# The attention rounds of a fused adaLN block: the two halves of k, the first quarters of q and their rotated parts at other steps of the round

## The chip, the cores and the metric

The kernel runs on one core of one Trainium2 chip. The metric is the device time of one execution in microseconds (us). Before the change three runs took 1324.26, 1326.85 and 1326.16 us, a median of 1326.16 us. A round is one of the sixteen passes of the causal attention described below; a step is one of a round's 36 parts. Names such as TensorE, VectorE, ScalarE, GpSimd and SyncE are the five engines (PE, DVE, ACT, POOL and SP in the profile).

## What is computed

The input is x of shape 4 x 1024 x 128. A first attention without a mask (stage A) and its projection are added to x, with modulated layer norms around them. Then comes the part that matters here, for each of 4 batch rows and each of 4 key heads h, with four query heads g that share the key head:

```
q = (x @ wq).reshape(b, t, 16, 64);  k = (x @ wk).reshape(b, t, 4, 64);  v = (x @ wv).reshape(b, t, 4, 64)
q = q * cos + neg_half(q) * sin;     k = k * cos + neg_half(k) * sin
scores = where(causal, q . k, -inf) / 8;  p = softmax(scores);  out = (p . v) @ wo
```

A routed mixture of 8 experts follows (top 2, a capacity of 512), and the sum goes out.

## The kernel before

The causal attention is 16 rounds, one for each batch row and key head, in this order, unrolled. A round has four query heads of nine steps, 36 steps in all. A step handles four 128 x 128 blocks of the lower triangle: TensorE makes their transposed scores (scoresB, L1199 and L1200, with a mask block at L1203), ScalarE takes exp (L917) and then a float16 copy, the "high" probabilities (L905), GpSimd subtracts that copy for the "low" half (L707), and five steps later TensorE multiplies both halves with the values (L1221 to L1223, twelve matmuls a step in two parts of six).

Beside this each round carries side work, an ordered list of some sixty entries. An entry is filled by TensorE into one of three PSUM banks, taken in turn, and read by VectorE or ScalarE out of it. TensorE may fill entry n only when entry n - 3 has been read (the function before). The entries are:

- max: a piece of the row maxima of a coming head (L1125, L1128), read by one VectorE reduction (L1608, or L1610 for a piece of two). EARLY puts pieces 0 to 5 at steps 4 to 8 of a head, LATE pieces 6 to 9 at steps 0 to 3 of the next head. After the last piece the ten are joined (L1634).
- row: the joined maxima, turned by TensorE at step 5 of a head (L1138) and copied by ScalarE (L897).
- k, q, r, v: the projections of the round that follows (L1113, three matmuls of 512 columns; v at L1107). k comes in two halves of 512 tokens, q in quarters (two pairs of heads, two halves of tokens); r is the quarter of q in the order that the rotation needs. VectorE reads a half of k with three instructions, each waiting for the one before (L1583, L1585, L1587), a quarter of q with one (L1597), of r with two (L1600, L1602).
- turn, out: the output projection of the round before (L1142, L1148). in2: the input of a coming batch row.

PROJ says at which step of a round each projection stands, OUTP the same for the output. side_work puts the entries of a step together, maxima first, then projection, output, in2 and row. HIGH_AT says at which step ScalarE makes the high half of the rotated k (0) and of the two pairs of q (1, 2), by high_half (L876, L878), LOW_AT at which step GpSimd makes the low half (low_half, L680, L682). SyncE then spreads them into the operands of the scores by DMA (spread_k, spread_q), between the rows of maxima (spread_row), in a fixed order.

TensorE's order inside a step is in pe_round: the scores, and then, where the step has one side entry, both parts of the values and the entry; where it has more, the first entry, a part of the values, the second entry, the other part, the rest:

```
if n == 1:
    order = parts[0:1] + parts[1:2] + todo
else:
    order = todo[0:1] + parts[0:1] + todo[1:2] + parts[1:2] + todo[2:]
```

VectorE reads the entries in the same order. At steps 3 and 5 of a head it also divides the finished output of a bank by its sums (norm: L1644, L1647), and in twelve places in rounds 0 to 8 it does a part of the second layer norm of a coming batch row (NORM_V; L1373, L1376, L1383, L1386, L1426), five of them at step 4 of rounds 0, 1, 2, 6 and 7. The first round's projections are made ahead of the rounds (PROLOGUE, which takes PROJ's entries in the order of their steps); round 15 has none.

Of the kernel before, what the change touches and what calls it, by code (L numbers as in the profile page):

```python
# [71 lines left out]
def reader(entry):  # L72
# [1 line left out]
    return READER[entry[0]]  # L74


PROJ = {0: ("k", 0), 1: ("k", 1), 3: ("q", 0, 0), 5: ("r", 0, 0), 7: ("q", 0, 1), 9: ("r", 0, 1), 11: ("v",),
        13: ("q", 1, 0), 15: ("r", 1, 0), 17: ("q", 1, 1), 19: ("r", 1, 1)}
OUTP = {21: ("turn", 0), 23: ("turn", 1), 25: ("turn", 2), 27: ("turn", 3), 30: ("out", 0), 33: ("out", 1)}

HIGH_AT = {4: 0, 12: 1, 22: 2}
LOW_AT = {5: 0, 15: 1, 25: 2}


INPUT_AT = {0: {29: (1, 0)}, 1: {31: (1, 1)}, 4: {29: (2, 0)}, 5: {31: (2, 1)}, 8: {33: (3, 0)}, 9: {29: (3, 1)}}
# [13 lines left out]
def side_work(it):  # L99
# [3 lines left out]
    for s in range(SPR):  # L103
# [4 lines left out]
        if not (last and h >= G - 2):  # L108
            now += [("max", h + 2, n) for n in EARLY.get(c, ())]
        if not last and s in PROJ:  # L110
            now.append(PROJ[s])
        if not first and s in OUTP:
# [3 lines left out]
        if c == ROW_AT and not (last and h == G - 1):  # L116
# [5 lines left out]

PROLOGUE = ([PROJ[s] for s in sorted(PROJ)] + [("max", G, n) for n in range(len(PIECES))] + [("row", G)]
            + [("max", G + 1, n) for c in sorted(EARLY) for n in EARLY[c]])
# [53 lines left out]
def build(nc, x, cT, wmod, w_qkvT, w_projT, b_proj, g1, g2, w_kv, w_o, router_w, router_b, w_exp, consts,  # L178
          cos_t, sin_t, out):
    ctx = ExitStack()  # L180
    with ctx:
# [406 lines left out]
        def _(pool):  # L588
# [86 lines left out]
            def low_half(c, n, p):  # L675

                t = (0, 1, 0)[c]
                pool.wait_ge(r_hi, 3 * n + c + 1)
                if c == 0:
                    pool.tensor_tensor(kC[0:HD, p, :], rp1[0:HD, t, :], kB[0:HD, p, :], ALU.subtract).then_inc(r_lo, 1)  # L680
                else:
                    pool.tensor_tensor(qlo[:, c - 1, :], rp1[:, t, :], qhi[:, c - 1, :], ALU.subtract).then_inc(r_lo, 1)  # L682
# [20 lines left out]
            def pool_round(it, p, first, last):  # L703
                for s in range(SPR):
                    pool.wait_ge(b_hi, it * SPR + s + 1)
                    r = s % RING
                    pool.tensor_tensor(pl[:, r, :], pf[:, r, :], ph[:, r, :], ALU.subtract).then_inc(lo_P, 1)  # L707
                    if s in LOW_AT and not last:
                        low_half(LOW_AT[s], it + 1, 1 - p)
                    if s in NORM_P.get(it, {}):  # L710
# [41 lines left out]
        def _(act):  # L752
# [112 lines left out]
            def vec_read_of(it, e):  # L865

                work = PROLOGUE if it < 0 else flat(side_work(it))
                own = [x for x in work if reader(x) == "V"].index(e)
                return own if it < 0 else start(it, "V") + own

            def high_half(c, n, p, read_at):

                act.wait_ge(side_V, read_at + 1)
                t = (0, 1, 0)[c]
                if c == 0:
                    act.activation(kB[0:HD, p, :], rp1[0:HD, t, :], ACT.Copy).then_inc(r_hi, 1)  # L876
                else:
                    act.activation(qhi[:, c - 1, :], rp1[:, t, :], ACT.Copy).then_inc(r_hi, 1)  # L878
# [28 lines left out]
            def act_round(it, p, first, last):  # L907
# [3 lines left out]
                for s in range(SPR):  # L911
# [5 lines left out]
                    act.activation(pf[:, s % RING, :], score_banks[s % SCORES], ACT.Exp).then_inc(b_exp, 1)  # L917
                    if s in HIGH_AT and not last:
                        c = HIGH_AT[s]
                        high_half(c, it + 1, 1 - p, vec_read_of(it, ROTATED[c]))  # L920
# [1006 lines left out]
```

## Time and profile before

| | us |
|---|---|
| three runs, median (lowest, highest) | 1326.16 (1324.26, 1326.85) |
| the profiled execution, its own time | 1324.32 |
| its span, first to last instruction | 1322.5 |
| TensorE busy (matmul) | 1116.2 |
| VectorE busy | 1053.8 |
| GpSimd busy | 998.5 |
| ScalarE busy | 872.8 |

All times of the trace are counted from the start of the span. In the timeline each line has the start, the length, the engine, the line of the kernel, the operation, and what is written and read; a bracket at the end gives how long the engine had been idle and what ended it. A matmul's end is modelled: the next one may start before it, so that a run of matmuls is timed by their starts. Rounds 0 to 15 fill the span from about 238 to 1110 us.

### The profile page before, as it was taken

What the parts mean: (1) busy time and instruction counts of PE and PEld (TensorE: products, weight loads), DVE (VectorE), ACT (ScalarE), POOL (GpSimd) and SP (SyncE); (2) the same over time, 40 slices, a digit from 0 to 9 for tenths busy, and PEclk for the clock granted to TensorE, in tenths of its full rate; (3) what the DMA queues carried; (4) which work ended last, traced back from release to release, by engine and by line L of the source; (5) the groups of instructions that cost most, each with busy time, mean ns of one, the idle gap of its engine ahead of it and who ended that gap; (6) DMA issues with size and microseconds to landing.
All of it is one profiled execution on the core that took longest, in us unless ns stands there. A gap on an engine that the chain in (4) does not pass through costs nothing.

```text
span 1322.5 us, 36076 instructions
## 1 busy us (share of the span) xinstructions
PE 1116.2 (84%) x14984; PEld 839.5 (63%) x14984; DVE 1053.8 (80%) x2180; ACT 872.8 (66%) x1508; POOL 998.5 (76%) x783
## 2 busy tenths in 40 slices
PE   4979895899999899999999999999999997600891
PEld 2768682566776667767677776776767776600881
DVE  6588765889888898989989889898898875592675
ACT  3656671698888688878888888887888894100330
POOL 3555874698898788989899898798888996226454
PEclk8889998899999899999999999999999999555996
DMA  6240013121222211213112131121211200022793
GB/s 219 50 140 2 2 44 86 42 77 43 71 55 56 61 38 52 58 60 77 38 52 54 49 87 43 53 61 42 77 38 26 62 3 2 0 88 74 219 303 145
DMA packets 49247, 90.85 MB, mean 69 GB/s; under 512 B 8896, under 2 KB 19136, under 8 KB 48832
## 3 DMA queue, kind: packets, MB, share of 16 engines
q1 hardware_dynamic: 46128, 81.21, 21.5%
q0 software_dynamic: 2960, 7.38, 2.1%
q8 instruction: 117, 1.92, 0.6%
q14 instruction: 42, 0.34, 0.1%
HBM read 43.96 MB, written 13.01 MB: 43 GB/s over the span
## 4 chain that ended last, share of the span: by engine, by line
PE 61%; DVE 20%; POOL 7%; issue 4%; SPq 3%; ACT 2%; DMA 2%; POOLq 0%; DVEq 0%; ACTq 0%
PE psT L1125 6%; PE psS L1200 5%; PE psS L1199 5%; PE psT L1113 5%; PE psS L1221 5%; PE psS L1222 5%; PE psS L1223 4%; PE psT L1148 3%; PE psO L1125 3%; PE psO L1200 3%; PE psO L1199 3%; DVE pmax L1608 2%; POOL rows_in L735 2%; DVE psT L1585 2%; DVE arena L1587 2%
## 5 line engine op out<-in xcount | busy, mean ns | idle before, releaser
L707 POOL TENSOR_TENSOR probs<-arena,probs 128x512 f16<-128x512 f32 x576 | 656.7, 1161 | 109.2 <-ACT probs L905 104.9
L905 ACT ACTIVATE probs<-arena 128x512 f16<-128x512 f32 x576 | 362.0, 628 | 14.1
L1221 PE MATMUL psS<-vb,probs 128*128 128x65 f16 x2304 | 302.9, 193 | 3.5 <-POOL probs L707 1.2
L1222 PE MATMUL psS<-vb,probs 128*128 128x64 f16 x2304 | 304.1, 194 | 0.0
L1223 PE MATMUL psS<-vb,probs 128*128 128x65 f16 x2304 | 302.2, 192 | 0.0
L917 ACT ACTIVATE arena<-psS 128x512 f32<-128x512 f32 x384 | 226.1, 589 | 105.9 <-PE psS L1203 59.1
L1221 PEld LDWEIGHTS psS<-vb,probs 128*128 128x128 f16 x2304 | 220.4, 97 | 71.6 <-issue 11.2
L1222 PEld LDWEIGHTS psS<-vb,probs 128*128 128x128 f16 x2304 | 215.7, 97 | 47.7 <-issue 0.5
L1608 DVE TENSOR_REDUCE pmax<-psT 128x1 f32<-128x512 f32 (+1 forms) x311 | 198.1, 641 | 28.9 <-PE psT L1128 14.1
L1223 PEld LDWEIGHTS psS<-vb,probs 128*128 128x128 f16 x2304 | 217.0, 99 | 0.0
L1125 PE MATMUL psT<-arena 128*128 128x512 f16 (+3 forms) x507 | 153.4, 323 | 8.6 <-DVE pmax L1608 4.9
L1200 PE MATMUL psS<-arena 65*128 65x512 f16 (+1 forms) x448 | 158.2, 353 | 0.0
L1199 PE MATMUL psS<-arena 128*128 128x512 f16 (+1 forms) x448 | 156.9, 350 | 0.0
L1608 DVE TENSOR_REDUCE pmax<-psO 128x1 f32<-128x512 f32 (+1 forms) x201 | 134.2, 667 | 23.9 <-PE psO L1125 16.2
L917 ACT ACTIVATE arena<-psO 128x512 f32<-128x512 f32 x192 | 112.5, 586 | 25.2 <-PE psO L1200 16.4
L1113 PE MATMUL psT<-arena,wkv 128*128 128x512 f16 x381 | 105.1, 386 | 20.8 <-DVE arena L1587 19.5
L647 POOL TENSOR_TENSOR probs<-arena,probs 128x1024 f16<-128x1024 f32 x32 | 69.4, 2172 | 55.8 <-ACT probs L847 55.7
L1199 PE MATMUL psO<-arena 128*128 128x384 f16 (+2 forms) x320 | 93.7, 293 | 0.0
L958 ACT ACTIVATE arena<-arena 128x256 f32<-128x256 f32 x40 | 16.7, 418 | 112.8 <-DVE arena L1841 112.7
L1125 PE MATMUL psO<-arena 128*128 128x512 f16 (+2 forms) x261 | 85.7, 341 | 5.4 <-DMA arena<-arena 4.6
L1200 PE MATMUL psO<-arena 65*128 65x384 f16 (+2 forms) x320 | 88.4, 295 | 0.0
L1128 PE MATMUL psT<-maskh,identh 128*128 128x128 bf16 x391 | 79.2, 220 | 0.0
(278 smaller groups left out, 2873.2 us busy)
## 6 DMA issues: line engine op xcount, KB each, us to landing
arena<-arena SPq DMA_DIRECT2D x240, 128.0 KB, 2.4
arena<-w_exp_dram SPq DMA_DIRECT2D x40, 384.0 KB, 4.1
arena<-xnT_d SPq DMA_DIRECT2D x16, 512.0 KB, 3.6
wkv<-w_d SPq DMA_DIRECT2D x16, 352.0 KB, 4.1
rows_in<-arena POOLq DMA_DIRECT2D x1, 2580.0 KB, 20.5
arena<-rows_in SPq DMA_DIRECT2D x40, 64.5 KB, 3.3
arena<-x_dram SPq DMA_DIRECT2D x4, 512.0 KB, 5.2
hres<-x_dram SPq DMA_DIRECT2D x4, 512.0 KB, 5.3
```

What stands on the lines that cost most here:

```text
L707: pool.tensor_tensor(pl[:, r, :], pf[:, r, :], ph[:, r, :], ALU.subtract).then_inc(lo_P, 1)
L905: act.activation(ph[:, s % RING, :], pf[:, s % RING, :], ACT.Copy).then_inc(b_hi, 1)
L917: act.activation(pf[:, s % RING, :], score_banks[s % SCORES], ACT.Exp).then_inc(b_exp, 1)
L1113: mm = pe.matmul(dst, wkv[:, p, c, w0:w0 + P], xs[:, p, a, h * 512:(h + 1) * 512], start=(k == 0), stop=(k == 2))
L1125: mm = pe.matmul(dst[:, k * w:(k + 1) * w], qA[:, p, g, i * P:(i + 1) * P], kC[:, p, h * 512:h * 512 + w], start=True, stop=not diag)
L1128: mm = pe.matmul(dst[:, (k + 1) * w - P:(k + 1) * w], identh[:, :], maskh[:, :], start=False, stop=True)
L1199: pe.matmul(dst, kA[:, p, j * P:(j + 1) * P], qA[:, p, g, i0 * P:(i0 + n) * P], start=True, stop=False)
L1200: mm = pe.matmul(dst, kB[0:HD + 1, p, j * P:(j + 1) * P], qB[0:HD + 1, p, g, i0 * P:(i0 + n) * P], start=False, stop=not diag)
L1221: pe.matmul(dst, high, vb[:, p, j, 0:OW], start=first, stop=False, skip_group_check=True)
L1222: pe.matmul(dst[:, 0:HD], high, vb[:, p, j, HD + 2:VW], start=False, stop=False, skip_group_check=True)
L1223: mm = pe.matmul(dst, low, vb[:, p, j, 0:OW], start=False, stop=last, skip_group_check=True)
L1608: ins = v.tensor_reduce(pmax[:, e[1] % 2, at[0]:at[0] + 1], src[:, 0:w], AX.X, ALU.max)
```

## The change

Three tables get other numbers. The first half of k stays at step 0; the second goes from step 1 to 2, the first quarter of q from 3 to 4, its rotated part from 5 to 6, the second quarter from 7 to 8; its rotated part stays at 9. ScalarE's high half of k goes from step 4 to 5, GpSimd's low half from 5 to 6. No instruction is added or taken out, and the order of the projections among themselves stays, so the prologue is unchanged. The order against the other entries changes: between the halves of k there are now two maxima and not one, and so on, and with it the bank of some entries.

```diff
-PROJ = {0: ("k", 0), 1: ("k", 1), 3: ("q", 0, 0), 5: ("r", 0, 0), 7: ("q", 0, 1), 9: ("r", 0, 1), 11: ("v",),
+PROJ = {0: ("k", 0), 2: ("k", 1), 4: ("q", 0, 0), 6: ("r", 0, 0), 8: ("q", 0, 1), 9: ("r", 0, 1), 11: ("v",),
         13: ("q", 1, 0), 15: ("r", 1, 0), 17: ("q", 1, 1), 19: ("r", 1, 1)}
 OUTP = {21: ("turn", 0), 23: ("turn", 1), 25: ("turn", 2), 27: ("turn", 3), 30: ("out", 0), 33: ("out", 1)}
 
-HIGH_AT = {4: 0, 12: 1, 22: 2}
-LOW_AT = {5: 0, 15: 1, 25: 2}
+HIGH_AT = {5: 0, 12: 1, 22: 2}
+LOW_AT = {6: 0, 15: 1, 25: 2}
```

## Rows read from the trace of the kernel before

**Rows 1.** The page's busy times: engine, us, share of the span, instructions.
```profile
PE 1116.2 (84%) x14984; PEld 839.5 (63%) x14984; DVE 1053.8 (80%) x2180; ACT 872.8 (66%) x1508; POOL 998.5 (76%) x783
```

**Rows 2.** TensorE's waits: who waited for whom, us in total, times, longest.
```profile
PE psT L1113 <- DVE arena L1587: 19.5, 17, 2.1
```

**Rows 3.** Timeline of TensorE, that wait in rounds 0 and 14.
```profile
245.07 0.82 PE L1113 MATMUL psT<-arena,wkv 128*128 128x512 f16 x3 [1.23 <-DVE arena L1587]
...
1016.53 0.82 PE L1113 MATMUL psT<-arena,wkv 128*128 128x512 f16 x3 [1.11 <-DVE arena L1587]
```

**Rows 4.** Timeline of TensorE, steps 0 to 9 of round 11.
```profile
846.58 0.39 PE L1125 MATMUL psT<-arena 128*128 128x512 f16 x1 [0.26 <-DVE pmax L1610]
846.99 0.81 PE L1113 MATMUL psT<-arena,wkv 128*128 128x512 f16 x3
847.82 0.38 PE L1199 MATMUL psS<-arena 128*128 128x512 f16 x1
848.03 0.38 PE L1200 MATMUL psS<-arena 65*128 65x512 f16 x1
...
849.54 0.38 PE L1199 MATMUL psO<-arena 128*128 128x512 f16 x1
...
850.56 0.38 PE L1199 MATMUL psS<-arena 128*128 128x512 f16 x1
...
852.67 0.82 PE L1113 MATMUL psT<-arena,wkv 128*128 128x512 f16 x3 [1.10 <-DVE arena L1587]
...
854.58 0.33 PE L1199 MATMUL psO<-arena 128*128 128x384 f16 x1
...
856.53 0.27 PE L1199 MATMUL psS<-arena 128*128 128x256 f16 x1
...
860.86 0.38 PE L1199 MATMUL psS<-arena 128*128 128x512 f16 x1
```

**Rows 5.** Timeline of VectorE, the same steps.
```profile
847.83 0.68 DVE L1583 TENSOR_TENSOR arena<-psT,trig 64x512 f32<-64x512 f32 x1
...
849.28 0.68 DVE L1587 TENSOR_TENSOR arena<-psT,arena 64x512 f32<-64x512 f32 x1
849.89 0.67 DVE L1608 TENSOR_REDUCE pmax<-psO 128x1 f32<-128x512 f32 x1
...
851.93 0.68 DVE L1587 TENSOR_TENSOR arena<-psT,arena 64x512 f32<-64x512 f32 x1
...
852.87 0.54 DVE L1608 TENSOR_REDUCE pmax<-psO 128x1 f32<-128x384 f32 x1
...
853.62 0.66 DVE L1597 TENSOR_TENSOR arena<-psT,trig 128x512 f32<-128x512 f32 x1
854.20 0.41 DVE L1647 TENSOR_TENSOR arena<-psS,oinv 128x256 f32<-128x256 f32 x1
```

**Rows 6.** Timeline of ScalarE and of GpSimd, the same steps.
```profile
854.69 1.04 ACT L876 ACTIVATE arena<-arena 64x1024 f16<-64x1024 f32 x1
...
856.34 2.42 POOL L707 TENSOR_TENSOR probs<-arena,probs 128x512 f16<-128x512 f32 x2 [2.52 <-ACT probs L905]
```

**Rows 7.** Timeline of VectorE and TensorE, norm work at step 4, rounds 2 and 1.
```profile
354.62 0.68 DVE L1426 TENSOR_TENSOR hres<-hres,rstd2a 128x512 f32<-128x512 f32 x1
...
298.49 1.21 DVE L1383 TENSOR_REDUCE st2a<-arena 128x8 f32<-128x1024 f32 x1
...
302.68 0.34 PE L1125 MATMUL psT<-arena 128*128 128x384 f16 x1 [0.52 <-DVE arena L1602]
```

**Rows 8.** Timeline of VectorE, TensorE and GpSimd, steps 24 and 25 of round 3.
```profile
440.42 4.37 DVE L1386 SCALAR_TENSOR_TENSOR st2b<-st2b,epsb 128x8 f32<-128x8 f32 x1
...
445.31 0.39 PE L1125 MATMUL psT<-arena 128*128 128x256 f16 x1 [4.69 <-DVE pmax L1608]
...
430.37 11.21 POOL L707 TENSOR_TENSOR probs<-arena,probs 128x512 f16<-128x512 f32 x10
...
443.61 1.15 POOL L707 TENSOR_TENSOR probs<-arena,probs 128x512 f16<-128x512 f32 x1
```

**Rows 9.** Busy time by stretch: TensorE, weights, VectorE, ScalarE, GpSimd; granted clock, DMA.
```profile
849.00:904.00 55.00, 53.49 (x766) 38.44 (x765) 48.16 (x92) 45.38 (x81) 47.22 (x39) 1.00 0.21 54
...
446.00:450.00 4.00, 4.00 (x30) 2.56 (x28) 3.42 (x6) 1.23 (x2) 1.16 (x1) 0.50 0.03 7
```

## The prediction, made before the changed kernel ran

> **What bounds the kernel now.** I first read the page's busy times [rows 1]: TensorE leads with 1116.2 us, but VectorE has 1053.8 and GpSimd 998.5, so a share alone names no limit. The stretches show the rounds: in the 55 us around round 11 TensorE is busy 53.49 us at a granted clock of 1.00, VectorE 48.16, GpSimd 47.22 [rows 9]. TensorE issues nearly without a hole, so a microsecond taken from its waits in a round is a microsecond of the kernel. The next view is therefore its waits. One group stands out: projections (L1113) that wait for the third instruction of a read of k (L1587), 17 times, 19.5 us [rows 2]. The timeline places them: two lie in the prologue, and one, of 1.1 to 1.2 us, stands in each of rounds 0 to 14, the rounds that carry projections [rows 3].
>
> Round 11 shows why [rows 4, 5]. Step 1 begins at 847.82, step 2 at 849.54, step 3 at 850.56. A projection and the half of the values behind it take 0.83 us of issue (846.99 to 847.82), three passes of 0.21 us (847.82 to 848.03) making 0.65 of it. So the second k is issued at 849.54 - 0.83 = 848.71, 0.89 after its step began. Step 3 is built alike but for a maximum of 384 columns, 0.05 us shorter: its quarter of q is due at 850.56 + 0.84 = 851.40. It starts at 852.67. The hole is 1.27 us (the bracket says 1.10 because the ends are modelled). It is there because this entry takes the bank of the second k, and VectorE was at that read until 852.6: a read of k is three chained instructions, 1.45 us from first to third (847.83 to 849.28), and two of them stand with one maximum between them.
>
> **The change part by part.** No instruction goes or comes, so every gain is a wait that ends earlier.
>
> *The second k at step 2.* Step 1 without it takes 1.72 - 0.65 = 1.07 us, so step 2 begins at 848.89. Its maximum and half of the values put the k at + 0.84, 849.73. Now it takes the bank of the first k (before, of a maximum). That read's third instruction starts at 849.28, and TensorE starts 0.74 us after such a start (851.93 to 852.67), at 850.02. So there is a new wait, 0.29 us. Step 3 begins 0.83 later, at 850.85.
>
> *The quarter of q at step 4.* Step 3 now looks like the old step 2, 1.02 us: step 4 begins at 851.87. The old step 4 ran from 852.67 + 0.84 to 854.58, 1.07 us with both halves of values; up to the quarter of q it takes 0.89, so this is due at 852.76. It needs the second k read. From k's issue to the first instruction is 0.84 (846.99 to 847.83), to the third 1.45, to the release 0.74: 850.02 + 3.03 = 853.05. VectorE is free for it: its two maxima behind the first k run from 849.89 and take 0.6 and 0.33 us, to 850.82, and the k arrives at 850.86. The wait is 0.29 us. Step 5 begins at 853.05 + 0.83 = 853.88 where it began at 854.58. **0.70 us is gained**: 1.27 becomes twice 0.29.
>
> *The rotated part at step 6, the second quarter at step 8.* VectorE is now late next. Step 5 took 1.95 us (854.58 to 856.53) and takes 1.30 without the rotated part; at step 6 scores, a maximum and half the values (0.95) put the rotated part at 856.13. It takes the bank of step 5's maximum. VectorE ends the second k at 852.31 + 0.61 = 852.92; a maximum, the joining and a reciprocal take 0.75 (852.87 to 853.62), the scaled output 0.5, then a maximum 0.6, the quarter of q 0.58 (853.62 to 854.20) and the maximum in question, starting at 855.33, released at 856.07. That is 0.06 us before it is needed: no wait, on a thin margin. Each further delay of VectorE would come through, so I let this term cost 0 to 0.3 us in a plain round. The second quarter at step 8 has two maxima ahead of it and is not late by the same count.
>
> *Rounds with norm work at step 4.* There VectorE has 0.6 us more (rounds 2 and 7) or a reduction of 1.21 us more (rounds 0, 1, 6) ahead of that maximum [rows 7]. For rounds 2 and 7 the thin margin becomes a wait of 0.54 us, and 0.16 us of gain is left. In the other three VectorE already makes TensorE wait again behind the rotated part (0.52 us by the bracket in round 1 [rows 7]); part of the new wait is one that was there anyhow. I bound each of them by - 0.5 and + 0.9 us and take + 0.5, nearer the upper end since that old wait disappears.
>
> *The high and low half of k.* The same copy of 1.04 us on ScalarE and the subtraction on GpSimd, one step on. On ScalarE the copy stood ahead of step 4's high probabilities; now these come first, the copy stands behind step 5's exp, and the row of maxima keeps its place behind it. GpSimd was idle 2.52 us for those probabilities [rows 6], so its catching up starts earlier, by about the 0.7 us that TensorE gains. What waits for k's halves is SyncE's three transfers (spread_k), queued ahead of a row that is only ready at step 14, and the first maximum that needs k, at step 22. That is 16 steps of cover, and I cost them nothing; without the cover each step of delay would stand in the first scores of a round.
>
> *The sum.* Plain rounds are 3, 4, 5 and 8 to 14: 10 x 0.70 = 7.0. Rounds 2 and 7: 0.3. Rounds 0, 1 and 6: 1.5. Together 8.8 us against the profiled 1324.32: 1315.5. The median of the runs, 1326.16, lies 1.8 higher and gives 1317.4; I forecast 1317.0. The bounds: 10 x 0.4 - 1.5 = 2.5 us of gain, and 19 us (15 x 1.27) if all of the wait went. I stay with the sum because the two new waits follow from durations of the same round.
>
> *One stall elsewhere.* In round 3 a VectorE instruction on 128 x 8 numbers in SBUF takes 4.37 us, ends with GpSimd's unbroken run (443.61 + 1.15), and costs TensorE 4.69 us [rows 8]; afterwards the granted clock is 0.50 [rows 9], the lower of its levels, 1.2 of 2.4 GHz. With about 5 us at half speed that is some 7.2 us. Whether it returns hangs on how its start falls against GpSimd's instructions; both move by the same 0.7 us, so I leave it in the sum. The Trainium skill, "SBUF — State Buffer", section "Who interferes with whom", says that a VectorE instruction with two SBUF inputs contends with a GpSimd one that reads SBUF, and that the one that issued second blocks until the first has finished. By that rule the wait would end with one GpSimd instruction, 1.1 us here; the row shows a wait past three of their ends, so the trace agrees on who blocks and not on how long.
>
> **The rivals.**
>
> *The stall of round 3 goes too* (0.23). For it: a shift of a tenth against GpSimd's 1.12 us beat (11.21 over ten [rows 8]) can decide. Against: the two move together. Then 1317.0 - 7.2 = 1309.8.
>
> *The wait is gone whole* (0.03): if VectorE released banks earlier than counted, 1326.2 - 19 = 1307. The chained read speaks against it.
>
> *Nothing is gained* (0.16). VectorE's work from step 0 to 9 is the same and nearly unbroken, so the old wait could come back whole behind the rotated part at step 6, or the stall of round 3 come once more in another place and take the gain: 1324.5 to 1326.5. Against: the idle between VectorE's reads in round 11, and the count above.
>
> *Slower* (0.09). Twelve pieces of the second norm run on VectorE in rounds 0 to 8, some with SBUF inputs beside a GpSimd that is seldom idle. If the moved phases add two more stalls of the kind of round 3, that is 2 x 7.2 - 8.8 = + 5.6: about 1331.8. It decides from the second on; one more only cancels the gain. Against: one of a dozen places does it now.
>
> **How the numbers follow.** The forecast has 0.49. The range goes from 1308.5 to 1323.5: it takes in the stall that goes (1309.8) and the forecast with its bounds (1326.16 - 2.5 = 1323.7 at the top), and leaves out most of no gain, the slower case and the whole wait gone. About 0.2%, or 2.7 us, is what a measurement of this kernel can tell from no change. Faster by more: 0.49 + 0.23 + 0.03 = 0.75; within: 0.16; slower: 0.09.
>
> **What would show it.** Right: in each of rounds 3 to 5 and 8 to 14 TensorE's bracket of 1.1 us is replaced by two small ones, at the second k and at the first quarter of q, both released by L1587; step 5 begins 0.7 us earlier after step 0; no bracket at the rotated part but in rounds 0, 1, 2, 6 and 7. Wrong: a bracket above 0.4 us at the rotated part (released by L1608) in plain rounds, or a stall as that of round 3 in another round. The prediction falls if the rounds keep their length although the bracket is gone.

## The result, and the profile after

The changed kernel takes 1315.28 us (median of four runs, 1314.48 to 1315.96) against 1326.47 us for the kernel before (1324.26 to 1326.85, a fourth run added to the three shown above). The ratio is 0.9916, with a 95% interval of 0.9902 to 0.993. The profiled execution took 1314.48 us with a span of 1312.7 us: 9.8 us less than before in both. It is the fastest of its four; the one before, at 1324.32 us, lies 0.06 us above the fastest run of its kernel. The forecast was 1317.0 us, 1308.5 to 1323.5, and faster.

The page of the changed kernel, to be read against [rows 1]:

```profile
PE 1115.0 (85%) x14984; PEld 837.8 (64%) x14984; DVE 1054.2 (80%) x2180; ACT 870.3 (66%) x1508; POOL 998.5 (76%) x783
```

The same work in the same number of instructions; only the span is shorter. What went is in TensorE's waits (who waited for whom, us in total, times, longest), to be read against [rows 2]:

```profile
PE psT L1113 <- DVE arena L1587: 3.5, 3, 2.1
PE psO L1113 <- DVE pmax L1608: 3.4, 5, 1.1
```

Of 17 waits for the third instruction of a read of k three are left, two of them the prologue's; the third, 0.86 us at the second k, is in round 0, where the first five steps have no values to multiply yet. In place of the others stand five, in the five rounds with norm work at step 4, released by a maximum (L1608).

Round 11 of the changed kernel, TensorE (start, length, engine, line, operation), answers to [rows 4]:

```profile
839.25 0.38 PE L1199 MATMUL psS<-arena 128*128 128x512 f16 x1
...
840.52 0.81 PE L1113 MATMUL psT<-arena,wkv 128*128 128x512 f16 x3
841.35 0.38 PE L1199 MATMUL psS<-arena 128*128 128x512 f16 x1
...
842.42 0.38 PE L1199 MATMUL psO<-arena 128*128 128x512 f16 x1
...
843.24 0.19 PE L1223 MATMUL psS<-vb,probs 128*128 128x65 f16 x1
843.56 0.82 PE L1113 MATMUL psT<-arena,wkv 128*128 128x512 f16 x3
844.40 0.38 PE L1199 MATMUL psS<-arena 128*128 128x512 f16 x1
...
845.42 0.38 PE L1199 MATMUL psS<-arena 128*128 128x512 f16 x1
...
846.61 0.82 PE L1113 MATMUL psT<-arena,wkv 128*128 128x512 f16 x3
847.45 0.33 PE L1199 MATMUL psO<-arena 128*128 128x384 f16 x1
...
848.75 0.27 PE L1199 MATMUL psS<-arena 128*128 128x256 f16 x1
...
849.71 0.81 PE L1113 MATMUL psO<-arena,wkv 128*128 128x512 f16 x3
...
893.21 0.38 PE L1199 MATMUL psS<-arena 128*128 128x512 f16 x1
```

and VectorE, which answers to [rows 5]:

```profile
842.82 0.68 DVE L1587 TENSOR_TENSOR arena<-psT,arena 64x512 f32<-64x512 f32 x1
...
844.42 0.68 DVE L1583 TENSOR_TENSOR arena<-psT,trig 64x512 f32<-64x512 f32 x1
...
845.87 0.68 DVE L1587 TENSOR_TENSOR arena<-psT,arena 64x512 f32<-64x512 f32 x1
...
848.88 0.68 DVE L1608 TENSOR_REDUCE pmax<-psO 128x1 f32<-128x512 f32 x1
```

The second k was due 0.84 us after its step began, at 843.26; it came at 843.56, 0.74 after L1587 started at 842.82. The quarter of q was due 0.89 after 845.42, at 846.31; it came at 846.61, 0.74 after 845.87. So there are two waits of 0.30 us where there was one of 1.27. Neither shows as a bracket, although the prediction named brackets as its sign: a matmul is recorded as ending up to 0.2 us after the next could be issued, so only 0.13 us of the first hole is left as idle time in the records (843.24 + 0.19 = 843.43, to 843.56), and the timeline puts no bracket on so little. Holes of this size are found by starts. Step 5 begins 6.10 us after step 1 (847.45 - 841.35); before it was 6.76 [rows 4]. The gain is 0.66 us.

Taking a round's length from its first score matmul to that of the next, round 11 took 53.96 us (893.21 - 839.25). Before, round 11 and round 12 began at

```profile
845.72 0.38 PE L1199 MATMUL psS<-arena 128*128 128x512 f16 x1
...
900.34 0.38 PE L1199 MATMUL psS<-arena 128*128 128x512 f16 x1
```

which makes 54.62 us. Worked out so for every round, the gains are 0.66 to 0.68 us in rounds 4, 5 and 8 to 14, 1.5 in round 3, 0.85 in round 1, 0.34 in round 6, 0.14 in rounds 2 and 7, - 0.14 in round 0 and none in round 15: together 8.8 us. Another 0.3 us lies before round 0 and 0.7 us after the rounds, in code that the change does not touch.

Round 3 keeps its stall, in VectorE, TensorE and GpSimd as in [rows 8]:

```profile
438.62 4.41 DVE L1386 SCALAR_TENSOR_TENSOR st2b<-st2b,epsb 128x8 f32<-128x8 f32 x1
...
443.55 0.40 PE L1125 MATMUL psT<-arena 128*128 128x256 f16 x1 [4.73 <-DVE pmax L1608]
...
428.61 11.21 POOL L707 TENSOR_TENSOR probs<-arena,probs 128x512 f16<-128x512 f32 x10
...
441.86 1.14 POOL L707 TENSOR_TENSOR probs<-arena,probs 128x512 f16<-128x512 f32 x1
```

Only the time at the lower clock behind it is shorter (busy times by stretch as in [rows 9], granted clock third from the end of the line), which is where round 3's other 0.9 us come from:

```profile
444.00:448.00 4.00, 4.00 (x43) 2.76 (x42) 3.61 (x7) 1.58 (x3) 1.07 (x1) 0.67 0.09 20
```

### The profile page after: what moved, and what is told of

Its sections match the earlier page's. It is cut to its first block, busy times and chain, and to the rows that moved or that the text cites. A ratio compares the mean times of both kernels' runs of the same rounds, so it can differ in the third digit from the quotient of the medians.

```text
span 1312.7 us, 36076 instructions
## 1 busy us (share of the span) xinstructions
PE 1115.0 (85%) x14984; PEld 837.8 (64%) x14984; DVE 1054.2 (80%) x2180; ACT 870.3 (66%) x1508; POOL 998.5 (76%) x783
## 4 chain that ended last, share of the span: by engine, by line
PE 60%; DVE 21%; POOL 7%; issue 4%; SPq 3%; ACT 2%; DMA 2%; POOLq 0%; DVEq 0%; ACTq 0%
PE psT L1125 6%; PE psS L1200 5%; PE psS L1199 5%; PE psS L1221 5%; PE psS L1222 5%; PE psT L1113 4%; PE psS L1223 4%; PE psT L1148 3%; PE psO L1200 3%; DVE pmax L1608 3%; PE psO L1199 3%; PE psO L1125 3%; POOL rows_in L735 2%; PE psO L1113 2%; DVE psT L1585 2%
## 5 line engine op out<-in xcount | busy, mean ns | idle before, releaser
L707 POOL TENSOR_TENSOR probs<-arena,probs 128x512 f16<-128x512 f32 x576 | 656.8, 1162 | 100.2 <-ACT probs L905 97.1
L905 ACT ACTIVATE probs<-arena 128x512 f16<-128x512 f32 x576 | 361.2, 627 | 14.5
L1608 DVE TENSOR_REDUCE pmax<-psT 128x1 f32<-128x512 f32 (+1 forms) x341 | 218.8, 645 | 26.1 <-PE psT L1128 13.5
L1125 PE MATMUL psT<-arena 128*128 128x512 f16 (+3 forms) x507 | 157.7, 329 | 8.3 <-DVE pmax L1608 5.2
L1608 DVE TENSOR_REDUCE pmax<-psO 128x1 f32<-128x512 f32 (+1 forms) x171 | 113.6, 664 | 18.5 <-PE psO L1125 12.3
L1113 PE MATMUL psT<-arena,wkv 128*128 128x512 f16 x336 | 92.8, 387 | 8.5 <-DVE arena L1587 3.5
L1125 PE MATMUL psO<-arena 128*128 128x512 f16 (+3 forms) x261 | 80.7, 328 | 5.1 <-DMA arena<-arena 4.7
L1128 PE MATMUL psT<-maskh,identh 128*128 128x128 bf16 x361 | 73.1, 220 | 0.0
```

Source lines behind the costliest of these rows:

```text
L905: act.activation(ph[:, s % RING, :], pf[:, s % RING, :], ACT.Copy).then_inc(b_hi, 1)
L1113: mm = pe.matmul(dst, wkv[:, p, c, w0:w0 + P], xs[:, p, a, h * 512:(h + 1) * 512], start=(k == 0), stop=(k == 2))
L1125: mm = pe.matmul(dst[:, k * w:(k + 1) * w], qA[:, p, g, i * P:(i + 1) * P], kC[:, p, h * 512:h * 512 + w], start=True, stop=not diag)
L1128: mm = pe.matmul(dst[:, (k + 1) * w - P:(k + 1) * w], identh[:, :], maskh[:, :], start=False, stop=True)
L1608: ins = v.tensor_reduce(pmax[:, e[1] % 2, at[0]:at[0] + 1], src[:, 0:w], AX.X, ALU.max)
```

## The experiments

The theory to be tested, called the bank theory: TensorE's wait is for a PSUM bank that VectorE still reads, and which entry waits follows from the order of the entries, three banks apart. Its rivals were that the distance between the two halves of k matters in itself, that thinning VectorE's reads matters, or that the later copies on ScalarE and GpSimd do. Executions differ by up to 3.6 us in the part before round 0 (the first score matmul stands between 236.95 and 240.56 us), so beside the medians I compare lengths of rounds, which do not carry that. Round 0 is an exception: experiment 9 edits rounds 2 and 3 alone, and its round 0 is still 1.06 us shorter than the changed kernel's (51.02 against 52.08), with a granted clock of 0.90 in its first part (237.84 to 241.00) against 0.68 (236.98 to 241.00). So a difference in round 0 is not laid to an edit here. Rounds are read from one traced execution of each kernel, and the runs of one kernel spread by 1.4 to 10.5 us. Each ratio is to runs of the kernel before that were taken beside it, with medians from 1325.55 to 1328.47 us, so it is the ratios that can be compared between experiments. Edits are against the changed kernel where nothing else is said.

**1. The projections alone.**

```diff
-HIGH_AT = {5: 0, 12: 1, 22: 2}
-LOW_AT = {6: 0, 15: 1, 25: 2}
+HIGH_AT = {4: 0, 12: 1, 22: 2}
+LOW_AT = {5: 0, 15: 1, 25: 2}
```

> The projections at the changed steps, the high and low half of k at their old steps 4 and 5. Bank theory (all of the gain is TensorE's wait for a bank that VectorE still reads; where ScalarE and GpSimd make the halves of k costs nothing): as the changed kernel, 1315.3 us within 1.5. Rival (the later halves keep ScalarE and GpSimd from waiting for the read of k, and part of the gain is theirs): 1318 to 1324 us, with a wait of ScalarE for L1587 in each round.

Measured: 1314.15 us (1309.02 to 1316.76), ratio 0.9905 (0.9873 to 0.9938). Round 11 takes 53.96 us, as with the whole change. But it is not the same in all rounds. Round 3 took

```profile
403.48 0.38 PE L1199 MATMUL psS<-arena 128*128 128x512 f16 x1
...
459.44 0.38 PE L1199 MATMUL psS<-arena 128*128 128x512 f16 x1
```

55.96 us against 60.31 with the change (458.87 - 398.56): its stall is short here, L1386 takes 0.94 us. And rounds 0, 1, 2 and 7 are 0.4 to 0.5 us longer than with the change. In round 2 VectorE's norm piece at step 4 (L1426) took 1.15 us where it takes 0.68 with the change; GpSimd was busy beside it. So the projections carry the gain of the plain rounds, and the moved halves of k change when GpSimd runs, which costs or gives where VectorE's norm pieces stand. The rival's sign, a wait of ScalarE for L1587 in each round, is absent: there is one, in the prologue, as in the changed kernel.

**2. The halves of k alone.** Against the kernel before:

```diff
-HIGH_AT = {4: 0, 12: 1, 22: 2}
-LOW_AT = {5: 0, 15: 1, 25: 2}
+HIGH_AT = {5: 0, 12: 1, 22: 2}
+LOW_AT = {6: 0, 15: 1, 25: 2}
```

> The projections at their old steps, the high and low half of k at the changed steps 5 and 6. Bank theory: as the kernel before, 1326.5 us within 1.5, with the bracket of 1.1 us at the first quarter of q in all 15 rounds. Rival (the halves carry part of the gain): 1318 to 1324 us.

Measured: 1325.76 us (1317.86 to 1328.35), ratio 0.999 (0.9972 to 1.0008). Round 11 takes 54.61 us (before 54.62), with the old wait:

```profile
854.45 0.82 PE L1113 MATMUL psT<-arena,wkv 128*128 128x512 f16 x3 [1.10 <-DVE arena L1587]
```

For the plain rounds the rival that gave ScalarE and GpSimd a share of the gain falls. In round 1 it does not. The halves alone make that round 0.72 us shorter (55.41 against 56.13), by as much as its small norm instruction L1386 becomes shorter, here before and in this experiment:

```profile
299.73 0.89 DVE L1386 SCALAR_TENSOR_TENSOR st2a<-st2a,epsb 128x8 f32<-128x8 f32 x1
...
302.91 0.17 DVE L1386 SCALAR_TENSOR_TENSOR st2a<-st2a,epsb 128x8 f32<-128x8 f32 x1
```

**3. The halves of k apart, q at its old steps.**

```diff
-PROJ = {0: ("k", 0), 2: ("k", 1), 4: ("q", 0, 0), 6: ("r", 0, 0), 8: ("q", 0, 1), 9: ("r", 0, 1), 11: ("v",),
+PROJ = {0: ("k", 0), 2: ("k", 1), 3: ("q", 0, 0), 5: ("r", 0, 0), 7: ("q", 0, 1), 9: ("r", 0, 1), 11: ("v",),
```

> Of the projections only the second half of k moves (step 1 to 2). Bank theory: the first quarter of q, still at step 3, now takes the bank of a maximum and does not wait; the second k waits 0.29 us for the first; a new wait of about 0.3 us comes at the maximum of step 7, behind the rotated part still at step 5. By that count 0.7 us are gained in a plain round and the time is 1316 to 1318 us. Rival (VectorE's reads have to be thinned out over the steps, so the moved quarters of q carry the gain): 1322 to 1327 us.

Measured: 1316.59 us (1313.65 to 1321.87), ratio 0.9939 (0.9916 to 0.9962). The time fell where the bank theory had it, and the median is out of the rival's 1322 to 1327. The first quarter of q, at step 3 as ever, does not wait at all: the bank it takes is now that of a maximum. Round 11 takes 54.05 us, 0.57 less than before. The new wait, though, is not at the maximum of step 7. It is at step 5, where the values write into a bank whose old content VectorE divides late, behind the reads of k and of the quarter of q:

```profile
849.36 0.19 PE L1221 MATMUL psS<-vb,probs 128*128 128x65 f16 x1 [0.23 <-DVE arena L1647]
```

My count had left that dependence out.

**4. The halves of k together, q at its new steps.** The second k back at step 1, all else as changed.

```diff
-PROJ = {0: ("k", 0), 2: ("k", 1), 4: ("q", 0, 0), 6: ("r", 0, 0), 8: ("q", 0, 1), 9: ("r", 0, 1), 11: ("v",),
+PROJ = {0: ("k", 0), 1: ("k", 1), 4: ("q", 0, 0), 6: ("r", 0, 0), 8: ("q", 0, 1), 9: ("r", 0, 1), 11: ("v",),
```

> The second half of k back at step 1, the quarters of q and the rotated part at the changed steps. Bank theory: the entry that waits for the second k is now the maximum of step 4, due 0.59 us before the release at 852.67 in the frame of round 11; 0.7 us of 1.27 are gained, 1315 to 1317 us. Rival (the distance of the two halves of k is what helps, as the name of the change has it): the wait of 1.1 us stays, 1324 to 1327 us.

Measured: 1316.99 us (1315.99 to 1318.75), ratio 0.9937 (0.9915 to 0.9959), and round 11 takes 53.96 us: the gain of a plain round is there in full, with the halves of k a single step apart. The wait is where the theory puts it, at step 4's maximum, which now takes the bank of the second k:

```profile
846.76 0.39 PE L1125 MATMUL psT<-arena 128*128 128x512 f16 x1 [0.43 <-DVE arena L1587]
```

By starts it is 0.6 us. The distance of the halves, the headline of the change, is not needed. Either move alone gives nearly all, since each puts another entry, due later, into the bank that the second k leaves.

**5. The read of the second k made longer.**

```diff
                 if kind == "k":
                     h = slice(e[1] * 512, (e[1] + 1) * 512)
+                    if e[1] == 1 and it > 0:
+                        v.tensor_reduce(spare[0:HD, it:it + 1], src[0:HD, :], AX.X, ALU.max)
```

> The changed kernel with one more VectorE reduction (64 x 512, some 0.6 us, its result not used) ahead of the read of the second half of k in 15 rounds. Bank theory (that read sets TensorE's wait at the first quarter of q): the wait grows from 0.3 to 0.9 us in each round, 15 x 0.6 = 9 us, about 1324. If VectorE has slack behind it or something else sets the wait: 1315 to 1317.

Measured: 1326.7 us (1325.35 to 1328.78), ratio 1.0011 (0.9997 to 1.0024). VectorE starts the added reduction at 852.65 and the read proper at 853.26, 0.61 us later; round 11 takes 54.56 us, 0.60 more than the changed kernel. Rounds 1, 2 and 4 to 14 are each 0.59 to 0.61 us longer, so what is added to this read TensorE waits for one to one. The median is 2.7 us above the 1324 expected; 2.3 us of the difference between the traced executions lie before and after the rounds, which the edit does not explain (the lines of this kernel are numbered one to three higher):

```profile
852.65 0.68 DVE L1585 TENSOR_REDUCE spare<-psT 64x1 f32<-64x512 f32 x1
853.26 0.67 DVE L1586 TENSOR_TENSOR arena<-psT,trig 64x512 f32<-64x512 f32 x1
...
855.43 0.82 PE L1114 MATMUL psT<-arena,wkv 128*128 128x512 f16 x3 [0.73 <-DVE arena L1590]
```

**6. q two steps later than before.** The second k is back at step 1.

```diff
-PROJ = {0: ("k", 0), 2: ("k", 1), 4: ("q", 0, 0), 6: ("r", 0, 0), 8: ("q", 0, 1), 9: ("r", 0, 1), 11: ("v",),
+PROJ = {0: ("k", 0), 1: ("k", 1), 5: ("q", 0, 0), 7: ("r", 0, 0), 9: ("q", 0, 1), 10: ("r", 0, 1), 11: ("v",),
-HIGH_AT = {5: 0, 12: 1, 22: 2}
+HIGH_AT = {5: 0, 13: 1, 22: 2}
```

> The second half of k at step 1, the first quarter of q at 5, its rotated part at 7, the second quarter at 9, its rotated part at 10; the high half of the first q at step 13. Bank theory: in a plain round only 0.22 us of wait is left, at the maximum of step 4, so about 1.0 of 1.27 us are gained, and rounds 0, 1, 2, 6, 7 lose less than in the changed kernel: about 1310 us, 1308 to 1313. Rival (VectorE's work as a whole limits the steps 0 to 10, so thinning cannot give more than the change has): 1314 to 1317 us.

Measured: 1310.88 us (1309.92 to 1312.48), ratio 0.9871 (0.9848 to 0.9895). The number is the expected one and the reason is not. Round 11 takes 54.18 us, longer than with the change and 0.44 less than before, where about 1.0 was expected: beside the small wait at step 4 the values of step 5 wait for VectorE's division again, by 0.42 us of bracket.

```profile
842.00 0.19 PE L1221 MATMUL psS<-vb,probs 128*128 128x65 f16 x1 [0.42 <-DVE arena L1647]
```

The time came from elsewhere: round 3 took 56.19 us instead of 60.31, its stall short as in experiment 1, and rounds 0, 1, 2, 6 and 7 gained 0.3 to 0.8 us each on the change. A median that lands on the forecast did not confirm the count here; the lengths of the rounds speak against it.

**7. Round 3's stall: another step.** The variance of the second norm (L1383, L1386) at step 22 of round 3.

```diff
-3: {24: ("d", 2)},
+3: {22: ("d", 2)},
```

> The changed kernel with round 3's piece of the second norm (variance, L1383 and L1386) at step 22 and not at 24. Chance theory (the small instruction L1386 comes in at the next end of a GpSimd instruction but for an unlucky moment): the wait shrinks to at most 1.2 us, TensorE's 4.7 us and the slow clock behind it go, 1308 us within 2. Backlog theory (it gets in only when GpSimd runs out of queued work): the wait stays at 4 us or more, 1314 to 1318 us.

Measured: 1317.13 us (1315.93 to 1317.31), ratio 0.9919 (0.9897 to 0.994). L1386 takes 3.03 us, from 437.23 to 440.26. GpSimd's run, in whose middle it was issued, ends at 430.13 + 10.11 = 440.24:

```profile
437.23 3.03 DVE L1386 SCALAR_TENSOR_TENSOR st2b<-st2b,epsb 128x8 f32<-128x8 f32 x1
...
430.13 10.11 POOL L707 TENSOR_TENSOR probs<-arena,probs 128x512 f16<-128x512 f32 x9
```

The nine instructions take 1.12 us each, so L1386 was issued some 0.4 us into one of them and two of their ends went by. The chance theory falls. The wait is also shorter than the 4 us or more of the backlog theory: GpSimd's run ended sooner after it.

**8. Round 3's stall: one input.**

```diff
-v.scalar_tensor_tensor(st[:, 3, :], st[:, 2, :], 1.0 / D, epsb[:, eps, :], ALU.mult, ALU.add).then_inc(n, 1)
+v.tensor_scalar(st[:, 3, :], st[:, 2, :], 1.0 / D, (LN_EPS, RMS_EPS)[eps], ALU.mult, ALU.add).then_inc(n, 1)
```

> The changed kernel with L1386 as an instruction with one SBUF input and two constants (times 1/128, plus the epsilon) in place of two SBUF inputs; the same numbers come out. If the second input from SBUF is what makes it wait for GpSimd: L1386 takes about 0.17 us in all places and the time is 1308 us within 2. If any VectorE instruction of that place waits (the second way: this form contends as well, or something else holds VectorE): about 4 us again, 1315 us within 1.5.

Measured: 1314.9 us (1314.6 to 1317.7), ratio 0.9907 (0.9883 to 0.9932); the instruction takes 4.43 us.

```profile
439.99 4.43 DVE L1386 TENSOR_SCALAR st2b<-st2b 128x8 f32<-128x8 f32 x1
```

A second input from SBUF is not needed for the wait. The Trainium skill, "SBUF — State Buffer", section "Who interferes with whom", names this form too among those that can take the pair of ports shared with GpSimd, so the run does not speak against the page's cause; it does show that this form is no way out.

**9. Round 3's stall: less queued on GpSimd.** One GpSimd piece of 2.36 us moved from round 3's step 8 to round 2's step 31.

```diff
-2: {18: ("scaled", 2)}, 3: {8: ("shifted", 2), 30: ("power", 2, 1)},
+2: {18: ("scaled", 2), 31: ("shifted", 2)}, 3: {30: ("power", 2, 1)},
```

> The changed kernel with one GpSimd piece of the second norm (2.36 us, L630) taken from round 3's step 8 to round 2's step 31. Backlog theory (L1386 waits at step 24 of round 3 because GpSimd's run behind that piece has no pause until its queued work is gone): GpSimd is 2.4 us less behind, its run has a pause before step 24, L1386 takes at most 1.2 us, and 4 to 7 us go: 1308 to 1311. Chance theory: the wait stays at about 4 us and the time at 1315.3 within 1.5.

Measured: 1312.68 us (1310.48 to 1315.41), ratio 0.9906 (0.9889 to 0.9923). The median is 1.7 us above the upper end of the range I gave. The six runs go from 1310.48, the traced one, up to 1315.41, where the chance theory had them, so whether the wait came in some of the others is not known. In the traced one it is gone. Round 3 takes 55.97 us (454.33 - 398.36), 4.3 less than with the change, and L1386 0.94:

```profile
438.41 0.94 DVE L1386 SCALAR_TENSOR_TENSOR st2b<-st2b,epsb 128x8 f32<-128x8 f32 x1
...
434.72 4.61 POOL L707 TENSOR_TENSOR probs<-arena,probs 128x512 f16<-128x512 f32 x4 [1.07 <-ACT probs L905]
439.29 2.12 POOL L682 TENSOR_TENSOR arena<-arena 128x1024 f16<-128x1024 f32 x1
```

GpSimd has caught up: it waited 1.07 us for ScalarE at 434.72, and L1386 gets in at the end of that run (434.72 + 4.61 = 439.33), although GpSimd's next instruction stood ready. The rest of TensorE's bracket, 1.25 us, is the variance itself and that wait.

**10. Both.** Experiment 9's edit, and the rest of q spread further behind the changed steps of k and of the first quarter of q.

```diff
-PROJ = {0: ("k", 0), 2: ("k", 1), 4: ("q", 0, 0), 6: ("r", 0, 0), 8: ("q", 0, 1), 9: ("r", 0, 1), 11: ("v",),
+PROJ = {0: ("k", 0), 2: ("k", 1), 4: ("q", 0, 0), 7: ("r", 0, 0), 9: ("q", 0, 1), 10: ("r", 0, 1), 11: ("v",),
-HIGH_AT = {5: 0, 12: 1, 22: 2}
+HIGH_AT = {5: 0, 13: 1, 22: 2}
```

> The edit before this one and, beside the changed steps of k and of the first quarter of q, its rotated part at step 7, the second quarter at 9, its rotated part at 10, the high half of the first q at 13. By the count of banks the plain rounds stay as in the changed kernel (two waits of 0.29 us), and the waits of 0.35 to 1.1 us at the rotated part in rounds 0, 1, 2, 6 and 7 go or fall below 0.5: some 3 us less than the edit before it, about 1306. If VectorE's work as a whole is the limit there: no gain on that edit.

Measured: 1308.25 us (1306.0 to 1312.03), ratio 0.9862 (0.9841 to 0.9882), below the change's own interval and that of experiment 9. It is the lowest here, but its interval overlaps that of experiment 6 (0.9848 to 0.9895). Some 3 us less than experiment 9 were expected; the median is 4.4 us lower, the rounds together 2.0. Round 11 takes 53.96 us as forecast, rounds 1, 2 and 7 gain 0.5 to 0.7 us each on the change, and the rounds together are 16.2 us shorter than before, against 8.8 for the change. The waits at the rotated part are gone. The two waits of 0.3 us are left, in round 0 as brackets of 0.9, and brackets of 0.4 and 0.2 us at a maximum in rounds 1 and 6.

## Why the prediction was right

**What bounds the kernel.** TensorE issues nearly without a hole in the rounds, and the hole of 1.27 us was VectorE's read of the second k. Experiments 3 and 4 show it by giving the bank of that read to another entry, experiment 5 by dose in the changed kernel: 0.61 us more of that read, 0.60 us more of round 11.

**The second k and the quarter of q.** Forecast: two new waits of 0.29 us, 0.70 us gained in a plain round. Measured: two of 0.30, and 0.66. The durations taken from one round before the change (0.84 from issue to read, 1.45 along the chain, 0.74 to release) came back in the round after it.

**The rotated part at step 6.** Forecast: needed at 0.06 us after its bank's release, no wait. Measured: released at 848.88 + 0.74 = 849.62, issued at 849.71 as due. The thin margin held.

**Norm work at step 4.** Forecast: 0.16 us of gain left in rounds 2 and 7, and 0.5 in each of rounds 0, 1 and 6, between - 0.5 and + 0.9. Measured: 0.14 twice, and - 0.14, 0.85 and 0.34, 1.05 together for the 1.5 forecast. The waits stand at the rotated part, where VectorE still reads the maximum whose bank it takes (here rounds 0, 1 and 7):

```profile
249.19 0.82 PE L1113 MATMUL psO<-arena,wkv 128*128 128x512 f16 x3 [0.71 <-DVE pmax L1608]
...
300.36 0.82 PE L1113 MATMUL psO<-arena,wkv 128*128 128x512 f16 x3 [1.08 <-DVE pmax L1608]
...
633.04 0.82 PE L1113 MATMUL psO<-arena,wkv 128*128 128x512 f16 x3 [0.35 <-DVE pmax L1608]
```

That these terms came out so near is in part luck. With the halves of k at their old steps (experiment 1) rounds 2 and 7 lose 0.33 us each, and rounds 0, 1 and 6 gain 0.2 together. The count had taken the norm piece of rounds 2 and 7 at the 0.68 us that it took before; it kept that length only because the halves had moved as well.

**The halves of k at nothing.** For the plain rounds experiments 1 and 2 show it: they keep and lose the gain without regard to these halves. For the other rounds this term failed: experiment 1 shows that, with the projections at their new steps, moving them cost 4.4 us in round 3 and gave some 0.5 us in each of rounds 1, 2 and 7, and with experiment 2 that most of round 1's 0.85 us came with them. Over all rounds the traced execution of experiment 1 is 2.6 us shorter than that of the change. The count had only asked who waits for the halves, not what GpSimd's moved work stands beside.

**The sum.** 8.8 us was forecast for the rounds and 8.8 was measured, with smaller parts cancelling: some 0.03 us less per plain round and 0.45 less in rounds 0, 1 and 6 together, against 0.8 us more in round 3 from a shorter time at the lower clock. That the two totals agree to a tenth is luck. The profiled executions differ by 9.84 us and the medians by 11.2; the 0.7 us after the rounds and the difference between medians and profiled runs are not traced further.

**The rivals.** That the wait goes whole, or comes back whole behind the rotated part, is out by the starts of round 11. The stall of round 3 stayed, as the forecast had it, with "both move by the same 0.7 us" as the ground. They did move together: L1386 was issued 10.05 us into GpSimd's run of ten before (440.42 - 430.37), 10.01 after (438.62 - 428.61), and 9.97 to 10.03 in experiments 2 to 5 and 8. That the stall stayed for this reason is not shown, and the rival's own reason, that a shift of a tenth against GpSimd's beat can decide, found no support: in experiments 7 and 9 L1386 was issued alike, 0.4 and 0.2 us into an instruction of GpSimd's, and it took 3.03 us in the one and 0.94 in the other. What differs is how long GpSimd had run without a pause, 25.9 us against 3.7. The price of 7.2 us was too high: without the stall round 3 is 4.3 us shorter than with the change (experiment 9), and TensorE keeps a bracket of 1.25 us there, which the price had counted in. No second such stall came in another round.

## What to carry to other kernels

Where a pipeline fills a few banks in turn and one reader is slow with some of them, ask for every step which entry takes the bank that is still being read, and put there one that is due late: in round 11 moving the second k alone gave 0.57 us, moving the quarters of q alone 0.66, and both 0.66. Such a plan can be counted ahead from a handful of starts and releases of one round, if every user of the slow engine is in the count: with VectorE's divisions left out, the counts of experiments 3 and 6 put the remaining wait at the wrong place. And work that is moved along off the critical path can cost or give elsewhere, as the halves of k did. A stall that happens once deserves its own look; here it was worth nearly half of what the change brought (4.3 us in round 3 of experiment 9, against 9.8 us of the span).

## What the runs showed of the hardware that was not expected

A VectorE instruction on 128 x 8 numbers in SBUF can wait for GpSimd through several of its instructions. In eight kernels (the two compared, and experiments 2 to 5, 7 and 8) L1386 of round 3 took 3.03 to 4.45 us and ended within 0.03 us of the end of GpSimd's unbroken run, past two or three ends of single instructions; where GpSimd had shortly before waited for ScalarE, it got in at the next end and took 0.93 to 0.94 us (experiments 1, 6, 9 and 10). That the one that issued second blocks until the other instruction has finished, as the Trainium skill has it ("SBUF — State Buffer", section "Who interferes with whom"), fits the second case and not the first.

Nor does queued work alone decide. In round 6 of the kernel before, the same line got in at an end inside GpSimd's run of seven (616.42 + 7.86 = 624.28) and took 0.72 us from 618.00, with two finished high halves waiting for GpSimd (by the ends of L905 and the starts of L707) where in round 3 there was one. Nor does the place within GpSimd's instruction decide: in round 8 of all twelve kernels L1386 was issued about 1.1 us into one, as in round 3 of seven of the eight, and took 0.17 us. In the changed kernel:

```profile
701.81 0.17 DVE L1386 SCALAR_TENSOR_TENSOR st2b<-st2b,epsb 128x8 f32<-128x8 f32 x1
...
698.41 4.60 POOL L707 TENSOR_TENSOR probs<-arena,probs 128x512 f16<-128x512 f32 x4 [0.50 <-ACT probs L905]
...
702.97 2.13 POOL L682 TENSOR_TENSOR arena<-arena 128x1024 f16<-128x1024 f32 x1
```

What separates the cases in all twelve kernels is how long GpSimd had run without a bracket when L1386 was issued: 25.9 to 30.1 us in the eight long waits, 8.3 us at most in all others. That sorts the cases and is not shown to be the cause; why GpSimd keeps VectorE out at some ends and not at others stays open. The long run ends when nothing is left for GpSimd: TensorE stands behind the wait, and ScalarE, whose copies GpSimd needs, is idle for want of scores. In round 3 of the changed kernel:

```profile
445.59 0.60 ACT L917 ACTIVATE arena<-psS 128x512 f32<-128x512 f32 x1 [5.87 <-PE psS L1200]
```

Experiment 9 shows that the wait of round 3 went when work was taken from GpSimd ahead of it, and experiment 7 that it was shorter two steps earlier; how this acts they do not show.
